# One attention and expert block on one core: the gate by a tangent, and a token tile finished and stored with each body of the second half

## What is computed

```python
xn  = layernorm(x)
s   = attention(xn, W_qkv, W_out)       # 32 query heads, 16 key/value heads of 64, alibi bias, causal
ffn = sum over each token's top 2 of 8 experts: weight * (gelu(xn @ w1 + b1) @ w2 + b2)
x   = x + s * silu(ffn)                 # silu(z) = z * sigmoid(z)
```

## Time and profile before

| | |
|---|---|
| runs (us) | 1255.94, 1253.67, 1255.06; median 1255.06 |
| the profiled execution | 1253.06 us, span 1251.1 us |
| granted PE clock, mean | 0.981 |
| busy | PE 92%, DVE 80%, ACT 75%, POOL 70% |
| DMA | 165.28 MB, 132 GB/s on average |
| HBM | read 15.76 MB, written 16.78 MB |

### The profile page before, as it was taken

One profiled execution on the slowest core, in us unless ns is written; L12 is line 12 of the kernel. 1 busy time (PEld: TensorE's weight loads), 2 busy tenths in 40 slices (PEclk: granted clock), 3 DMA queues, 4 the chain that ended last, 5 costly groups with the idle time before them and its releaser, 6 DMA issues. The chain is left out here.

```text
span 1251.1 us, 52908 instructions
## 1 busy us (share of the span) xinstructions
PE 1154.0 (92%) x17226; PEld 912.5 (73%) x17226; DVE 1005.5 (80%) x3099; ACT 939.0 (75%) x1807; POOL 878.3 (70%) x1086
## 2 busy tenths in 40 slices
PE   2579999999999999987999779999999999999994
PEld 0357777777777777766888657777777777777873
DVE  8778888888888888764777648888888888888885
ACT  2468888888888888775666458888888888888884
POOL 9048888888888888875000058888888888888885
PEclk9989999999999999999999979999999999999997
DMA  8326666666666666644433456555555555555663
GB/s 243 158 57 144 143 147 151 143 143 144 144 144 144 144 143 143 147 107 86 87 90 86 94 129 141 136 135 134 134 134 134 134 134 134 134 134 134 138 139 95
DMA packets 286161, 165.28 MB, mean 132 GB/s; under 512 B 174994, under 2 KB 274674, under 8 KB 285428
## 3 DMA queue, kind: packets, MB, share of 16 engines
q1 hardware_dynamic: 281972, 155.63, 54.7%
q0 software_dynamic: 4096, 8.40, 2.3%
HBM read 15.76 MB, written 16.78 MB: 26 GB/s over the span
## 5 line engine op out<-in xcount | busy, mean ns | idle before, releaser
L781 POOL TENSOR_TENSOR t_lo<-stage 128x512 f16<-128x512 f32 x640 | 654.4, 1038 | 148.7 <-ACT stage L1180 144.5
L1392 DVE CUSTOM_DVE_ANT_0 stage<-ps,kmask 128x512 bf16<-128x512 f32 (+3 forms) x1024 | 466.2, 488 | 110.7 <-PE ps L878 91.9
L1180 ACT ACTIVATE stage<-ps,slope 128x512 f32<-128x512 f32 (+1 forms) x768 | 456.8, 620 | 126.8 <-PE ps L913 80.7
L904 PE MATMUL ps<-q_st,k_st 128*128 128x256 f16 (+3 forms) x1024 | 302.5, 301 | 4.0 <-DMA k_st<-stage 1.8
L936 PE MATMUL outs<-v_sp,stage 128*128 128x65 f16 x2560 | 283.3, 194 | 12.2 <-DVE stage L1422 9.0
L938 PE MATMUL outs<-v_sp,stage 128*128 128x64 f16 x2560 | 283.1, 194 | 0.0
L940 PE MATMUL outs<-v_sp,t_lo 128*128 128x65 f16 x2560 | 283.0, 194 | 0.0
L878 PE MATMUL ps<-k_st,stage 128*128 128x512 f16 (+3 forms) x1024 | 252.8, 304 | 14.9 <-DVE spread L1392 7.6
L936 PEld LDWEIGHTS outs<-v_sp,stage 128*128 128x128 bf16 x2560 | 239.4, 98 | 21.5 <-issue 11.2
L938 PEld LDWEIGHTS outs<-v_sp,stage 128*128 128x128 bf16 x2560 | 236.5, 98 | 8.9 <-issue 0.3
L940 PEld LDWEIGHTS outs<-v_sp,t_lo 128*128 128x128 f16 x2560 | 236.5, 98 | 0.0
(11 more groups left out here) (205 smaller groups left out, 2702.1 us busy)
## 6 DMA issues: line engine op xcount, KB each, us to landing
k_st<-stage SPq DMA_DIRECT2D x256, 128.0 KB, 2.4
q_st<-stage SPq DMA_DIRECT2D x256, 128.0 KB, 2.4
q_st<-stage SPq DMA_DIRECT2D x256, 64.0 KB, 2.1
k_st<-stage SPq DMA_DIRECT2D x128, 64.0 KB, 2.1
slot_y<-stage SPq DMA_DIRECT2D x40, 128.0 KB, 2.0
X<-in_L_attn_inputs SPq DMA_DIRECT2D x8, 512.0 KB, 8.0
slot_x<-att SPq DMA_DIRECT2D x2, 2048.0 KB, 8.7
wx_raw<-in_L_ffn_w SPq DMA_DIRECT2D x64, 64.0 KB
```

The lines of the kernel that those rows point to most:

```text
L781: pool.tensor_tensor(t_lo[r], t_p[r], upper(t_p[r]), ALU.subtract).then_inc(s[f"lo{u % NG}"], 1)
L904: pe.matmul(d, k[:, 0, at], q[:, 0, seen], start=(c0 == 0), stop=False, skip_group_check=True)
L1180: e = act.activation(t_p[r][:, c0:c1], S_ps[u % 2][:, c0:c1], ACT.Exp, scale=slope[:, bass.ds(pair_index(n) * 2 * SLOTS + sl * 2 + h, 1)])
L1392: ins = dve.tensor_tensor_reduce(junk[h][:, c0:c0 + w], M_ps[h][:, c0:c0 + w], kmask[:, SEQ - w:SEQ], -1.0 / 1024, 3e38, ALU.add, ALU.min, ...
```

## The change

1. Four new tasks are put into the second list of ORDER, all with offset -3, so they work on the tile of the body three windows back: T on ACT, `tangents`, tanh(0.5 * mix) of one tile into one of two 128x128 f32 buffers (the row buffers of the first half, seen as f32); U on POOL, `gate_tile`, mix = mix * att; X on DVE, `gated`, buffer = (buffer + 1) * mix; Z on DVE, `with_input`, X = 0.5 * buffer + X. A fifth, H on SP, `hand_out`, stores the tile (64 KB). They act on tiles 0 to 27 (`finishes`: below LAST = 28).
2. The silu activations, `finish`, its calls on POOL and DVE and the three stores are gone.
3. The last four tiles are finished at the end: one 128x512 tanh on ACT, (tanh + 1) * mix on DVE ahead of the last `accumulate`, which `leave_bodies` leaves out by `late` and which is called by hand; then in two pieces of two tiles a product with att, an addition to X and a store of 128 KB.

The diff, cut to its core:

```diff
         "ACT": [
-            ("K0", 1, 0), ("V0", 0, 4), ("E0", 0, 11), ("E1", 0, 15), ("Q0", 1, 22), ("E2", 0, 26), ("C1", 0, 33),
+            ("K0", 1, 0), ("V0", 0, 4), ("E0", 0, 11), ("E1", 0, 15), ("Q0", 1, 22), ("E2", 0, 26), ("T0", -3, 26), ("C1", 0, 33),
...
         "DVE": [
...
-            ("B2", 1, 59), ("B3", 1, 64), ("B4", 1, 70), ("B5", 1, 74), ("O0", -2, 76), ("Q1", 1, 80),
-            ("N0", 0, 86), ("B6", 1, 96),
+            ("B2", 1, 59), ("B3", 1, 64), ("B4", 1, 70), ("B5", 1, 74), ("O0", -2, 76), ("Q1", 1, 80), ("X0", -3, 80),
+            ("N0", 0, 86), ("Z0", -3, 86), ("B6", 1, 96),
...
         "POOL": [
...
-            ("L3", 0, 49), ("I1", 1, 56), ("G0", 0, 63), ("L4", 0, 65), ("D0", 1, 72), ("L5", 0, 78), ("L6", 0, 85),
+            ("L3", 0, 49), ("I1", 1, 56), ("G0", 0, 63), ("L4", 0, 65), ("U0", -3, 65), ("D0", 1, 72), ("L5", 0, 78), ("L6", 0, 85),
...
         "SP": [
-            ("K0", 1, 13), ("A0", -1, 26), ("K1", 1, 36), ("Q0", 1, 49), ("A1", -1, 67), ("Q1", 1, 94),
+            ("K0", 1, 13), ("A0", -1, 26), ("K1", 1, 36), ("Q0", 1, 49), ("A1", -1, 67), ("H0", -3, 67), ("Q1", 1, 94),
...
+        g_now = [row_now[par][:, :].bitcast(F32) for par in range(2)]
+        g_last = xg_more[:, :].bitcast(F32)
...
+        def finishes(n):
+            return not isinstance(n, int) or n - HALF < LAST, n - HALF
...
+            def hand_out(n, _par, _):
+                done, t = finishes(n)
+                if done:
+                    sp.wait_ge(s["fin"], t + 1)
+                    sp.dma_start(ot[:, bass.ds(t, 1), :], X[:, bass.ds(t, 1), :]).then_inc(s["outd"], 16)
...
-            for c, (t0, t1) in enumerate(PIECES):
-                sp.wait_ge(s[f"fin{c}"], 1)
-                sp.dma_start(ot[:, t0:t1, :], X[:, t0:t1, :]).then_inc(s["outd"], 16)
-            sp.wait_ge(s["outd"], 16 * len(PIECES))
+            for c in range(2):
+                sp.wait_ge(s["fin"], LAST + c + 1)
+                tiles = slice(LAST + c * QT // 2, LAST + (c + 1) * QT // 2)
+                sp.dma_start(ot[:, tiles, :], X[:, tiles, :]).then_inc(s["outd"], 16)
+            sp.wait_ge(s["outd"], (LAST + 2) * 16)
...
+            def gate_tile(n, par, _):
+                done, t = finishes(n)
+                if done:
+                    pool.wait_ge(s["gate_t"], t + 1)
+                    pool.wait_ge(s["acc"], n)
+                    pool.tensor_tensor(tile_of(mix, t), tile_of(mix, t), tile_of(att, t), ALU.mult).then_inc(s["gate_u"], 1)
...
-            finish(pool, 0)
...
-            def gates(c):
-                g = out_chunk(mix, c)
-                act.activation(g, g, ACT.Silu).then_inc(s["silu"], 1)
+            def tangents(n, par, _):
+                done, t = finishes(n)
+                if done:
+                    act.wait_ge(s["added"], t + 1)
+                    need(act, "fin", t - 1)
+                    act.activation(g_now[par], tile_of(mix, t), ACT.Tanh, scale=0.5).then_inc(s["gate_t"], 1)
...
+            act.wait_ge(s["added"], NT)
+            act.activation(g_last[:, :], tile_of(mix, LAST, QT), ACT.Tanh, scale=0.5).then_inc(s["gate_t"], 1)
...
-                if isinstance(n, int) and n == BODIES - 1:
-                    finish(dve, 1)
...
-            run_bodies(dve, "DVE", tasks, HALF, BODIES)
-            leave_bodies("DVE", tasks, HALF, BODIES)
-            finish(dve, 2)
+            def gated(n, par, _):
+                done, t = finishes(n)
+                if done:
+                    dve.wait_ge(s["gate_u"], t + 1)
+                    g = g_now[par]
+                    dve.scalar_tensor_tensor(out=g, in0=g, scalar=1.0, in1=tile_of(mix, t), op0=ALU.add, op1=ALU.mult)\
+                       .then_inc(s["gate_p"], 1)
+
+            def with_input(n, par, _):
+                done, t = finishes(n)
+                if done:
+                    dve.wait_ge(s["gate_p"], t + 1)
+                    dve.wait_ge(s["xend"], 64)
+                    xx = tile_of(X, t)
+                    dve.scalar_tensor_tensor(out=xx, in0=g_now[par], scalar=0.5, in1=xx, op0=ALU.mult, op1=ALU.add)\
+                       .then_inc(s["fin"], 1)
+
+            run_bodies(dve, "DVE", {**tasks, "X": gated, "Z": with_input}, HALF, BODIES)
+            leave_bodies("DVE", tasks, HALF, BODIES, late=[BODIES - 1])
+            dve.wait_ge(s["gate_t"], LAST + 1)
+            dve.scalar_tensor_tensor(out=g_last[:, :], in0=g_last[:, :], scalar=1.0, in1=tile_of(mix, LAST, QT), op0=ALU.add,
+                                     op1=ALU.mult).then_inc(s["gate_p"], 1)
+            accumulate(BODIES - 1, (BODIES - 1) % UNROLL, 0)
+            dve.wait_ge(s["gate_p"], LAST + 1)
+            dve.wait_ge(s["acc"], BODIES)
+            for c in range(2):
+                g = g_last[:, c * QT // 2 * D:(c + 1) * QT // 2 * D]
+                t = LAST + c * QT // 2
+                dve.scalar_tensor_tensor(out=g, in0=g, scalar=0.5, in1=tile_of(att, t, QT // 2), op0=ALU.mult, op1=ALU.mult)\
+                   .then_inc(s["gate_p"], 1)
+                dve.wait_ge(s["gate_p"], LAST + c + 2)
+                dve.tensor_tensor(tile_of(X, t, QT // 2), tile_of(X, t, QT // 2), g, ALU.add).then_inc(s["fin"], 1)
```

More of the change, by code:

```diff
@@ L274, in build @@
         names = """x0 x1 x2 x3 wq0 wq1 wo sm ident consts small
-            stat rstd norm xnD xnA xtr xhi xlo b1tr b1 gate gate_w whi wlo attz var topexp gap silu
+            stat rstd norm xnD xnA xtr xhi xlo b1tr b1 gate gate_w whi wlo attz var topexp gap
             picked ranked routed zeros ready0 ready1 rhi sent0 sent1 got00 got01 got10 got11 weighed0 weighed1 added
@@ L278, in build @@
             xload0 xload1 hmm0 hmm1 gelu0 gelu1 hhi hlo0 hlo1 ymm yout ystore0 ystore1
-            gated0 gated1 gated2 rd0 rd1 nrm0 nrm1 op acc ta0 ta1 ah0 ah1 al0 al1 rows
+            gate_t gate_u gate_p rd0 rd1 nrm0 nrm1 op acc ta0 ta1 ah0 ah1 al0 al1 rows
             turnc0 turnc1 crow0 crow1 copied
@@ L282, in build @@
             qmm0 qmm1 qh0 qh1 ql0 ql1 kmm kh kl vmm vh vl
-            fin0 fin1 fin2 outd""".split()
+            fin outd""".split()
         s = {n: sem("s_" + n) for n in names}
@@ L444, in build, with tile_of @@
         LAST = NT - QT
[L445 to L461, removed]
+        LATER = 3
+        def finishes(n):
+            return not isinstance(n, int) or n - HALF < LAST, n - HALF
+        def tile_of(m, t, k=1):
+            return m[:, bass.ds(t, k), :].rearrange("p t d -> p (t d)")
         def sent_with(n):
@@ L509, in _ @@
             xt = x.rearrange("b (t p) d -> p (b t) d", p=P)
+            ot = out.rearrange("b (t p) d -> p (b t) d", p=P)
             def inputs(c):
@@ L623, in _ @@
                 sp.dma_start(X[:, 8 * c:8 * c + 8, :], xt[:, 8 * c:8 * c + 8, :]).then_inc(s["xend"], 16)
-            run_bodies(sp, "SP", stacks, HALF, BODIES)
-            leave_bodies("SP", stacks, HALF, BODIES)
-            ot = out.rearrange("b (t p) d -> p (b t) d", p=P)
-            for c, (t0, t1) in enumerate(PIECES):
-                sp.wait_ge(s[f"fin{c}"], 1)
-                sp.dma_start(ot[:, t0:t1, :], X[:, t0:t1, :]).then_inc(s["outd"], 16)
-            sp.wait_ge(s["outd"], 16 * len(PIECES))
+            def hand_out(n, _par, _):
[3 more added lines that the diff above has]
+                    sp.dma_start(ot[:, bass.ds(t, 1), :], X[:, bass.ds(t, 1), :]).then_inc(s["outd"], 16)
+            run_bodies(sp, "SP", {**stacks, "H": hand_out}, HALF, BODIES)
+            leave_bodies("SP", stacks, HALF, BODIES)
+            for c in range(2):
[3 more added lines that the diff above has]
+            sp.wait_ge(s["outd"], (LAST + 2) * 16)
         @block.gpsimd
@@ L802, in _ @@
                 pool.wait_ge(s[f"ystore{k}"], NBLK // 2 * 16)
-            fetches = {"L": lo_part, "I": fetch_ready, "D": fetch, "G": add_expert}
+            def gate_tile(n, par, _):
[4 more added lines that the diff above has]
+                    pool.tensor_tensor(tile_of(mix, t), tile_of(mix, t), tile_of(att, t), ALU.mult).then_inc(s["gate_u"], 1)
+            fetches = {"L": lo_part, "I": fetch_ready, "D": fetch, "G": add_expert, "U": gate_tile}
             enter_bodies("POOL", fetches, HALF, BODIES)
@@ L1141, in v_hi_part @@
                                ACT.Copy, scale=1.0 / WS).then_inc(s["vh"], 1)
-            def gates(c):
-                g = out_chunk(mix, c)
-                act.activation(g, g, ACT.Silu).then_inc(s["silu"], 1)
-            def out_hi(n, _, sl):
[L1150 to L1154, removed]
+            def tangents(n, par, _):
[4 more added lines that the diff above has]
+                    act.activation(g_now[par], tile_of(mix, t), ACT.Tanh, scale=0.5).then_inc(s["gate_t"], 1)
+            def out_hi(n, _, sl):
                 act.wait_ge(s[f"nrm{sl}"], n + 1)
@@ L1160, in out_hi @@
                 act.copy(by_head(a16[sl][:, 0:SEQ]), values_of(sl)).then_inc(s[f"ah{sl}"], 1)
-                if final:
-                    gates(2)
```

(4 more changed lines are left out.)

## The result

The changed kernel takes **1408.1 us** (median of 4 runs, 1407.4 to 1412.3). The kernel before takes 1254.4 beside it (4 runs, 1251.5 to 1255.9). The ratio is 1.123, 95% interval 1.121 to 1.126. Forecast was 1248.2, a little faster; it came out 154 us slower, far outside the range.

A forecast was written before the change was run, and what follows sets the result against it. PE was taken to set the pace, 15.6 us a body. From 1253.06 us profiled, 7.2 off for the end and 0.3 added gave 1246.2; plus 2.0 to the median, 1248.2 us, range 1246.0 to 1253.2.

The forecast's parts named there:

- Body, DVE: X and Z add 0.58 to 1.12 us to each of 28 bodies, against 1.11 of cover; counted 0.
- The weighing against the Trainium skill: On X and Z's placing: trace taken to agree on contention but not blocking, as two additions ran side by side 3.8 us.
- DVE blocked by POOL: Rival: X and Z each wait out one low part of POOL, 1.55 us a body, 1291 us; chance 0.07.
- End, DVE: After PE's last matmul: DVE's last accumulation starts at once, four 128x256 operations follow; gain 4.4 us.
- End, DMA: Last output store: 128 KB lands in 2.0 us instead of 4.8; gain of another 2.8 us.
- End, ACT and POOL: At the end: table load, two gates and POOL's two operations go; PE waited for none, counted nothing.
- Body, POOL: U in each body takes 0.46 us, perhaps 0.7 shared with DVE, against slack of 0.9; counted 0.
- Body, ACT: T in each body costs about 0.4 us, 0.22 of it in idle time, the rest harmless; counted 0.
- the rival on it: Rival: tanh not loaded with the exponential, two table loads a body, some 10 to 50 us slower; chance 0.02.
- Body, SP: H delays query and key DMAs by 0.5 to 1.1 us a body; counted 0.3 us in all 28 bodies.

The follow-up runs named there:

- z_in_place: Against moved: Z put back behind the normalisation, X stays moved; 1247.3 us, ratio 0.994.
- moved: Against the changed kernel: X and Z at places of DVE's list where POOL pauses, one body later, H with them; 1246.2 us, ratio 0.994.
- one_input: Against the changed kernel: X and Z of the body replaced by same-size statistics operations with one SBUF input each; 1246.5 us, ratio 0.994.
- pool_gives_way: Against the changed kernel: POOL waits for X ahead of low part 5 and for Z ahead of low part 7; 1253.0 us, ratio 1.000.
- eight_columns: Against the changed kernel: X and Z of the body work on 8 of their 128 columns, both inputs kept; 1407.2 us, ratio 1.122.
- x_in_place: Against moved: X put back where the changed kernel has it, Z and H stay moved; 1276.5 us, ratio 1.018.
- fetches_apart: Against the changed kernel: POOL's two indirect fetches taken out from between the low parts and issued earlier; 1345.9 us, ratio 1.074.

## Why the prediction was wrong

- **"Body, DVE" failed, at its upper bound.** It priced contention at 3.16 ns a column and so at 0.56 an operation; they took 2.07 and 3.42. The number came from dividing the 5.67 us of DVE's addition in the earlier trace rows by its columns, which assumes that both engines slow each other down evenly. The ends say otherwise. POOL's L461 began at 1236.19 and took 5.62, so it ended at 1241.81. DVE's, begun at 1238.03, ended at 1243.70, 1.89 us later, and 1.89 us is what 1792 columns take at 1.04 ns with nobody in the way (1.86). It had stood still until POOL was done. The pair before it, in the kernel before, reads the same way:

```profile
1235.33 2.66 DVE L459 TENSOR_TENSOR att<-att,mix 128x1792 f32<-128x1792 f32 x1
...
1232.11 4.00 POOL L459 TENSOR_TENSOR att<-att,mix 128x1792 f32<-128x1792 f32 x1 [1.83 <-ACT mix L1146]
```

  POOL's ends at 1236.11, DVE's at 1237.99, 1.88 later. And POOL's L461, which began in that time, took 5.62 where its like took 4.00: DVE kept it out in its turn. (1.80 of waiting for DVE's end and 4.00 of work are 0.18 more than the 5.62 that it took, and no run tests this pair by itself, so this half is argued from the rows alone.) "Side by side for 3.8 us" was two engines taking turns. The evidence that I held against blocking was evidence for it.

- **The weighing against the Trainium skill** went the wrong way for that reason, and because it took in a part of the page only. The Trainium skill (SBUF — State Buffer, section "Who interferes with whom") says that two SBUF inputs on VectorE contend with a GpSimd instruction that reads SBUF; it calls the shared ports an exclusive lock, and describes blocking for an instruction's whole length for the modes that take both ports. The same page of the Trainium skill, in its section "SBUF: two separate sides", states that blocking for two SBUF inputs as well: whichever starts first has the ports for its whole instruction. The trace agrees that the engine is blocked. It differs on the length: 3.42 and 3.49 us, through three instructions of GpSimd and more.

- **The rival "DVE blocked by POOL" named the mechanism** and was 1291 us against 1408. It mis-sized the wait as one low part (1.04), with three errors. The wait lasts a run of two or three low parts: X and Z cost 5.49 instead of 2.66. The earlier trace rows leave out the run that stood beside X's place already in the kernel before, where X was expected at 1025.9:

```profile
1025.29 2.04 POOL L781 TENSOR_TENSOR t_lo<-stage 128x512 f16<-128x512 f32 x2
```

  The first wait decides which run the second meets (z_in_place). And the lower clock was not in it, nor in any other term of the sum. With the measured durations its own sum gives 28 x (5.49 - 1.11) - 7 = +116; the 2.2 us a body at the lower clock adds 62, and the idle time that PE really got, 3.8 and not 4.4, takes back 15: +163, against the 159 between the two profiled executions. A chance of 0.07 for it was too little.

- **The range** left the whole blocked case outside, on one reading of two rows. The bound of a term that counts 28 times rested on it; either end of it that is off by 1 us moves the sum by 28.

- **"End, DVE", "End, DMA", "End, ACT and POOL" held:** 7.1 of 7.2 us, landing 2.0, 128x256 in 0.42, last accumulation 0.04 after PE. `moved` gives the total that these steps forecast: 1246.2 beside a kernel before of 1253.9, 7.7 less, against 6.9 forecast.

- **"Body, POOL" and "Body, ACT" held:** U takes 0.45 and T 0.31. No table load stands in the body, so the rival on it (0.02) fell. one_input and moved leave T and U where they are and run at 15.6 a body.

- **"Body, SP" cannot be told apart** from noise: 0.3 us forecast; H was never measured alone.

## What to carry to other kernels

When two engines overlap and both are long, do not divide by columns: compare the end of the one with the end of the other. If the later one ends its own undisturbed duration after the earlier, it was locked out, and then a short operation pays for whatever run it meets, not for its own size. Put an operation with two inputs in SBUF where the other engine pauses, or give it one input; the same work cost 0.28 us there and 3.4 a few rows on, and a wait that stops the bound engine can cost more than itself.

## What the runs showed of the hardware

- A DVE operation with two SBUF inputs ended 0.15 to 0.16 us after the end of POOL's run of back-to-back elementwise operations: runs of two (1.94 and 2.07 us, z_in_place 0.98), three (3.42) and four (3.49 of a run of 4.02). 8 columns waited as long as 128 and ended 0.03 to 0.04 us after the run. POOL's low parts stayed at 1.0 us. With one SBUF input: 0.28, in the same places.
- The exception, Z at 0.55 us in pool_gives_way and once in z_in_place, is open: what lets DVE in between two of POOL's operations there was not found.
- Whether an indirect fetch of POOL keeps DVE out too was not tried by itself. In eight_columns Z was ready 0.24 us before a fetch ended (1009.85) and did not come through.
- A gap of 3.7 us in PE is followed by more than 3 us at a granted clock of 0.50; with the gaps of x_in_place, 0.7 at most, the clock stayed at 1.00. fetches_apart lies between: one gap of 1.9 to 2.3 us in nearly every body, and a granted clock of 0.95 on average over 800 to 1200. The clock stays up behind a gap of 2.30 us and falls behind the next one, of 2.00, so the length of the gap alone does not decide. Rows of both:

```profile
1010.45 0.38 PE L892 MATMUL ps<-k_st,stage 128*128 128x128 f16 x2 [2.30 <-DVE spread L1404]
1012.00:1013.00 1.00, 1.00 (x27) 0.82 (x24) 1.00 (x8) 0.87 (x2) 0.10 (x1) 1.00 0.66 153
...
1028.61 0.39 PE L892 MATMUL ps<-k_st,stage 128*128 128x128 f16 x2 [2.00 <-DVE spread L1404]
1029.70:1033.10 3.40, 3.40 (x44) 2.61 (x42) 2.15 (x11) 1.58 (x3) 2.05 (x4) 0.51 0.49 116
```
